# A two-layer transformer block: attention in equal chunks of 512 columns, and a mixture of experts that computes only the chosen token-expert pairs

## The chip, the cores and the metric

One core of one Trainium2 chip runs the whole program in one launch. The metric is the device time of one execution in microseconds (us), the median over several runs. Shapes: 8 batches of 512 tokens with 128 features, 16 heads of 8 features, 8 experts with 512 hidden units, two experts for each token.

## The reference, cut to what matters

```python
q, k1, k2, v = (split_heads(x @ W.T) for W in (Wq, Wk1, Wk2, Wv))
a = softmax(causal(q k1^T * SCALE)) - sigmoid(lam)[h] * softmax(causal(q k2^T * SCALE))
a = a / maximum(sum(abs(a), -1), 1e-6)
x = layernorm(x + merge_heads(a @ v) @ Wo.T)

xn = layernorm(x) * gamma + beta
w, idx = top_k(softmax(xn @ router_w.T / 1.5), 2)
wdense = sum(one_hot(idx, 8) * w[..., None], -2)
h = silu(einsum('btd,edf->betf', xn, W1))
y = einsum('betf,efd->betd', h, W2)
x = layernorm(x + einsum('bte,betd->btd', wdense, y) + x)
```

The reference computes all 8 experts for every token and weighs six of them with zero.

## The kernel before, in words

**One static order for each engine.** The kernel is written by hand, one instruction stream for each engine, with semaphores between them. `run` calls `body(b, stages)` for b from -1 to 9. In a body, every engine walks through 64 slots (`for slot in range(UNITS)`), and does in each slot what a lag of its own assigns to it. An engine executes in order, so a wait in one slot holds back all that stands behind it on that engine.

**Attention.** A unit is one head and one tile of 128 queries; its score strip is 128 to 512 columns wide (causal), so 16 heads x 4 tiles = 64 units a batch, one in each slot. PE writes the two score strips into PSUM (`scores`, two units deep; L853, and the causal mask by L855), DVE takes each strip's negated maximum (`neg_max`, L723), ACT takes the exponential with its row sum (L491), and POOL makes the difference of the two softmaxes in place: a scaling (L441) and then a subtraction (L445), for each unit. `inv_l2` (DVE L714) and `lam_l1` (POOL L437) are made once for four units. PE transposes the difference (L883), ACT copies it out of PSUM (`diffT`, L499), PE multiplies with the values (L872). DVE sums absolute values (`abs_sum`, L734, two units in one instruction), and every four units makes `guard` (L623) and its reciprocal (L740). Scores are stored as three bfloat16 parts: SP writes `parts` to DRAM (L390) and reads them back as `stack` (L398), nine transfers for each of four groups of heads, for the batch that follows.

**The rest of the layer in side slots.** `SIDE` gives slots to tasks. "prep" tasks are for batch b+1 (transpose of x, projections L773, values), "post" tasks for batch b-1: division, output projection, two norms, transposed `xnT`, router logits, 16 small routing steps on DVE (`route`), and then the experts: for each of 8 experts 4 `hidden` tasks (PE L803, one 128x512 product; ACT tanh L537; DVE `hT` L686) and 4 `expert` tasks (PE L809, 4 accumulating products of 128x128; DVE adds the gated result into `acc`, L698). An fp32 product is two PE instructions. Tasks of slots above 63 run as "late" in the body after. The weights of all experts lie in SBUF (4 MB, loaded once at L384). PSUM banks `side0` and `side1` alternate between the side tasks; in the last bodies, the four score banks join them.

**SP** issues all transfers, in this order in a body: x for the next batch, x for the residual, `parts`, `stack`, and the output. `stack` of group g waits until the scores of that group in the running batch are done.

Of the kernel before, what the change touches and what calls it, by code (L numbers as in the profile page):

```python
# [29 lines left out]
FP32, BF16 = mybir.dt.float32, mybir.dt.bfloat16  # L30
ALU, ACT, AX = mybir.AluOpType, mybir.ActivationFunctionType, mybir.AxisListType

B, T, D = 8, 512, 128
# [4 lines left out]
NF = F // P  # L38
UNITS = NH * NT
QUAD = 4  # L40
QUADS = UNITS // QUAD
NG = NH // QUAD
TILE_ORDER = (1, 0, 2, 3)
# [8 lines left out]
LAG_DIFF = QUAD + LAG_EXP  # L52
LAG_TRANS = LAG_DIFF + 2
LAG_COPY = LAG_TRANS + 1
LAG_ABS = LAG_DIFF + 2
LAG_DEN = LAG_ABS + 2
LAG_PV = LAG_COPY + QUAD
LAG_SIDE = 1

SIDE = {}
POST_SLOTS = {"spread": 8, "den_T": 9, "divide": 11, "out_proj": 13, "norm1": 15, "norm2": 18,
              "xn_T": 19, "logits": 21, "router_exp": 22}
FIRST_EXPERT_SLOT = 20
EXPERT_TASKS = (1, 2, 1, 1, 1, 1, 1, 1, 0, 1, 1, 1, 1, 1, 1, 1)
PREP_SLOTS = (24, 29, 36, 42, 43)


def tile_of(q):  # L70

    return TILE_ORDER[q % NT]


def _place():

    def put(slot, *task):
        SIDE.setdefault(slot, []).append(task)

    for name, slot in POST_SLOTS.items():  # L80
        put(slot, "post", name)
    tasks = []
    for e in range(E + 1):
        for n in range(NF):
            if e < E:
                tasks.append(("post", "hidden", e, n))
            if e:
                tasks.append(("post", "expert", e - 1, n))
    slot = FIRST_EXPERT_SLOT
    while tasks:  # L90
        for _ in range(min(EXPERT_TASKS[slot % len(EXPERT_TASKS)], len(tasks))):
            put(slot, *tasks.pop(0))
        slot += 1
    put(slot + 1, "post", "norm3")
    put(slot + 3, "post", "finish")
# [4 lines left out]
_place()  # L100
ROUTE_STEPS, ROUTE_PLACES = 16, 4
# [3 lines left out]
PSUM_TASKS = ("den_T", "out_proj", "xn_T", "logits", "hidden", "expert", "x_T", "proj", "values")  # L105

STORED = (0, 1, 2, 0, 1)
# [7 lines left out]
class Signal:  # L115


    def __init__(self, sem, per_batch, step=1):
        self.sem, self.per, self.step = sem, per_batch, step

    def after(self, batch, n):

        value = (batch * self.per + n) * self.step + CREDIT
        return max(value, 1) if isinstance(value, int) else value


def build(nc, x, wqT, wk1T, wk2T, wvT, woT, lam, gamma, beta, rwT, w1, w2, out):
    ctx = ExitStack()  # L130
    with ctx:
# [8 lines left out]
        def signal(name, per_batch, step=1):  # L140
            signals.append(Signal(ctx.enter_context(nc.semaphore(name)), per_batch, step))
            return signals[-1]

# [14 lines left out]
        w1_sb = sb("w1_sb", [P, E, F])  # L158
        w2_sb = sb("w2_sb", [P, E, NF, D])

# [8 lines left out]
        scratch = nc.dram_tensor("parts_dram", [3, NH, len(STORED), HD, T], BF16).ap()  # L169
        stack = sb("stack", [STACK, 3, NH, T], BF16)  # L170


        neg_max = sb("neg_max", [P, 2, QUAD, 2])
        sums = sb("sums", [P, 4, 2, QUAD])
        inv_l2 = sb("inv_l2", [P, 2, QUAD])
        lam_l1 = sb("lam_l1", [P, 2, QUAD])
        exps = sb("exps", [P, 2, 2, QUAD, T])
        diff = exps[:, :, 1, :, :]
        diffT = sb("diffT", [P, 2, QUAD, T])
        abs_sum = sb("abs_sum", [P, 2, QUAD])  # L180
        guard = sb("guard", [P, QUAD])
        inv_den = sb("inv_den", [P, NT, NH])
        inv_wide = sb("inv_wide", [P, NT, NH, HD])
# [5 lines left out]
        r1 = sb("r1", [P, NT, D])  # L189
        x1 = sb("x1", [P, NT, D])  # L190
# [14 lines left out]
        gates = sb("gates", [P, NT, E])  # L205
        tanh_sb = sb("tanh_sb", [P, 2, T])
        hT = sb("hT", [P, 2, NF, T])
        x1_twice = sb("x1_twice", [P, NT, D])
# [10 lines left out]
        CONSTS = 9 + E  # L219
        weights_in = ctx.enter_context(nc.semaphore("weights_in"))  # L220
        experts_in = ctx.enter_context(nc.semaphore("experts_in"))
# [16 lines left out]

        score_done = signal("score_done", 2 * UNITS)
        max_done = signal("max_done", 2 * UNITS)  # L240
        exp_done = signal("exp_done", 2 * UNITS)
        inv_l2_done = signal("inv_l2_done", QUADS)
        lam_l1_done = signal("lam_l1_done", QUADS)
        scaled_done = signal("scaled_done", UNITS)
        diff_done = signal("diff_done", UNITS)
        abs_done = signal("abs_done", 2 * QUADS)
        trans_done = signal("trans_done", UNITS)
        diffT_copied = signal("diffT_copied", UNITS)
        pv_done = signal("pv_done", QUADS)
        den_done = signal("den_done", 2 * QUADS)  # L250

        res_loaded = signal("res_loaded", 1, 16)
        post_psum = signal("post_psum", 4)
        expert_psum = signal("expert_psum", E * (NF + NT))
# [17 lines left out]
        tanh_done = signal("tanh_done", E * NF)  # L272
        hidden_done = signal("hidden_done", E * NF)
        expert_done = signal("expert_done", E * NT)
# [4 lines left out]
        def reader(task):  # L279
# [5 lines left out]
                "hidden": (hidden_done, NF * task[2] + task[3] + 1) if name == "hidden" else None,  # L285
# [28 lines left out]
        def psum_of(task):  # L314

            if task[1] in ("hidden", "expert"):
                return expert_psum
# [593 lines left out]
```

## Time and profile before

| what | us |
|---|---|
| median of 3 runs | 1229.79 (1222.33 to 1231.21) |
| the profiled execution, its device time | 1223.18 |
| its span in the trace | 1221.3 |
| PE, DVE, ACT, POOL busy | 1103.2, 1044.4, 915.2, 834.0 |

The span is what the hardware profiler saw from first to last instruction; 1.9 us of the execution lie around it. Instructions that wait on a semaphore, and those that issue a transfer, are not counted as busy.

### The profile page before, as it was taken

To read this page: it belongs to the slowest core of one execution; us is meant where nothing else is said; L and a number is where in the kernel's file an instruction comes from. 1 tells how busy PE (TensorE), PEld (TensorE's weight loads), DVE (VectorE), ACT (ScalarE), POOL (GpSimd) and SP (SyncE) were. 2 spreads that over 40 slices of the span, in tenths; PEclk is the share of its full clock that TensorE was granted. 3 is DMA by queue.
4 is the path that set the end of the run, shared out by engine and by line. 5 is a ranking of instruction groups with operands and counts; after the bars stand their busy time and mean duration, and the time that the engine had idled before them with its cause. 6 is when DMAs were issued, how large, how long until landed. Compare 5 with 4: busy or idle time off the path is not lost.

```text
span 1221.3 us, 29361 instructions
## 1 busy us (share of the span) xinstructions
PE 1103.2 (90%) x8786; PEld 725.7 (59%) x8786; DVE 1044.4 (86%) x2722; ACT 915.2 (75%) x2882; POOL 834.0 (68%) x1245
## 2 busy tenths in 40 slices
PE   3788869999899989999899997999899998999897
PEld 1355536666556655666556665666556665566565
DVE  1688788988999899999999899999999999898664
ACT  1688868888688877888688876888678886787232
POOL 2599976776768757877667776777677777677100
PEclk8577779999999999999999999999999999999899
DMA  7503400232005200142003300052002410000000
GB/s 213 126 14 80 99 1 3 62 82 48 1 14 118 70 2 2 36 110 57 1 14 86 89 15 1 21 125 57 1 2 57 89 48 1 19 1 2 1 10 9
DMA packets 62142, 54.66 MB, mean 45 GB/s; under 512 B 6050, under 2 KB 59938, under 8 KB 61986
## 3 DMA queue, kind: packets, MB, share of 16 engines
q1 hardware_dynamic: 61986, 52.78, 17.8%
q8 instruction: 73, 1.20, 0.4%
q14 instruction: 83, 0.68, 0.2%
HBM read 37.03 MB, written 15.73 MB: 43 GB/s over the span
## 4 chain that ended last, share of the span: by engine, by line
PE 66%; DVE 18%; issue 7%; POOL 4%; ACT 2%; SPq 1%; DMA 1%; DVEq 0%; POOLq 0%; ACTq 0%
PE side L809 14%; PE side L803 13%; PE trans L883 12%; PE scores L853 8%; PE heads L872 7%; DVE neg_max L723 6%; PE scores L855 4%; DVE abs_sum L734 3%; PE scores L803 2%; PE scores L809 2%; POOL exps L445 2%; PE side L773 2%; DVE hT L686 1%; DVE xh L566 1%; POOL exps L441 1%
## 5 line engine op out<-in xcount | busy, mean ns | idle before, releaser
L491 ACT ACTIVATE exps<-scores,neg_max 128x256 f32<-128x256 f32 (+3 forms) x1024 | 537.9, 529 | 97.5 <-DVE neg_max L723 80.8
L723 DVE TENSOR_REDUCE neg_max<-scores 128x1 f32<-128x256 f32 (+3 forms) x1024 | 448.7, 479 | 72.8 <-PE scores L855 69.3
L445 POOL TENSOR_TENSOR exps<-exps 128x384 f32<-128x384 f32 (+3 forms) x512 | 444.7, 868 | 42.7
L441 POOL TENSOR_SCALAR exps<-exps,inv_l,lam_l 128x384 f32<-128x384 f32 (+3 forms) x512 | 313.6, 613 | 141.2 <-DVE inv_l L714 138.4
L853 PE MATMUL scores<-stack 72*128 72x256 bf16 (+3 forms) x1024 | 274.1, 314 | 17.5 <-DMA stack<-parts_dram 13.5
L809 PE MATMUL side<-w_sb,hT 128*128 128x128 f32 x1816 | 253.6, 283 | 29.5 <-DVE acc L698 18.1
L883 PE MATMUL trans<-ident,exps 128*128 128x128 f32 x1280 | 254.9, 300 | 22.8 <-ACT diffT L499 19.4
L499 ACT ACTIVATE diffT<-trans 128x384 f32<-128x384 f32 (+3 forms) x512 | 223.4, 436 | 52.9 <-PE trans L883 52.1
L809 PEld LDWEIGHTS side<-w_sb,hT 128*128 128x128 f32 x1816 | 222.6, 192 | 63.7 <-DVE acc L698 29.9
L803 PE MATMUL side<-xnT,w_sb 128*128 128x512 f32 x458 | 247.2, 621 | 1.8 <-ACT xnT L526 1.0
L883 PEld LDWEIGHTS trans<-ident,exps 128*128 128x128 f32 x1280 | 150.4, 147 | 134.7 <-issue 102.5
L855 PE MATMUL scores<-causal_bf,ident_bf 128*128 128x128 bf16 x1024 | 216.5, 228 | 0.0
L491 ACT ACTIVATION_READ_ACCUMULATOR exps<-scores,neg_max 128x1 f32 x1024 | 210.7, 206 | 0.0
L734 DVE TENSOR_REDUCE abs_sum<-exps 128x2 f32<-128x512 f32 (+3 forms) x256 | 206.9, 808 | 1.7 <-POOL exps L445 1.7
L686 DVE SCALAR_TENSOR_TENSOR hT<-tanh_sb,side 128x512 f32<-128x512 f32 x229 | 155.8, 680 | 36.3 <-ACT tanh_sb L537 34.5
L537 ACT ACTIVATE tanh_sb<-side 128x512 f32<-128x512 f32 x229 | 136.1, 594 | 48.0 <-PE side L803 44.8
L853 PEld LDWEIGHTS scores<-stack 72*128 72x128 bf16 x1024 | 108.2, 106 | 64.1 <-ACT exps L491 22.8
L872 PE MATMUL heads<-diffT,v_sb 128*32 128x128 f32 x2560 | 139.2, 291 | 0.0
L872 PEld LDWEIGHTS heads<-diffT,v_sb 128*32 128x32 f32 x2560 | 51.0, 109 | 122.2 <-ACT diffT L499 61.4
L855 PEld LDWEIGHTS scores<-causal_bf,ident_bf 128*128 128x128 bf16 x1024 | 105.4, 103 | 7.7
L437 POOL TENSOR_TENSOR lam_l<-sums,lam_all 128x4 f32<-128x4 f32 x128 | 25.9, 203 | 91.1 <-ACT exps L491 90.7
L803 PEld LDWEIGHTS side<-xnT,w_sb 128*128 128x128 f32 x458 | 69.3, 191 | 15.0 <-DVE hT L686 2.7
(94 smaller groups left out, 685.2 us busy)
## 6 DMA issues: line engine op xcount, KB each, us to landing
stack<-parts_dram SPq DMA_DIRECT2D x288, 96.0 KB
parts_dram<-parts SPq DMA_DIRECT2D x104, 128.0 KB, 2.4
x_in<-x_dram SPq DMA_DIRECT2D x8, 256.0 KB, 4.5
w_sb<-w_dram SPq DMA_DIRECT2D x1, 2048.0 KB, 9.1
x_res<-x_dram SPq DMA_DIRECT2D x8, 256.0 KB, 4.5
o_dram<-y_out SPq DMA_DIRECT2D x8, 256.0 KB, 3.4
wq_sb<-wqT_dram SPq DMA_DIRECT2D x1, 64.0 KB
wq_sb<-wk1T_dram SPq DMA_DIRECT2D x1, 64.0 KB
```

The source lines that it names most:

```text
L441: nc.gpsimd.tensor_scalar(diff[:, q % 2, j, 0:w], exps[:, q % 2, 1, j, 0:w], inv_l2[:, q % 2, j:j + 1], lam_l1[:, q % 2, j:j + 1], ALU.mul ...
L445: nc.gpsimd.tensor_tensor(diff[:, q % 2, j, 0:w], diff[:, q % 2, j, 0:w], exps[:, q % 2, 0, j, 0:w], ALU.subtract).then_inc(diff_done.sem, 1)
L491: nc.scalar.activation(exps[:, q % 2, k, j, 0:w], scores[:, u % 2, k, 0:w], ACT.Exp, bias=neg_max[:, q % 2, j, k:k + 1], accum_out=sums[:, ...
L499: nc.scalar.activation(diffT[:, q % 2, j, 0:w], trans[:, 0:w], ACT.Copy)\
L723: nc.vector.tensor_reduce(neg_max[:, q % 2, j, k:k + 1], scores[:, u % 2, k, 0:w], AX.X, ALU.max, negate=True).then_inc(max_done.sem, 1)
L734: nc.vector.tensor_reduce(abs_sum[:, q % 2, j - 1:j + 1], diff[:, q % 2, j - 1:j + 1, 0:w], AX.X, ALU.add, apply_absolute_value=True).then ...
L803: last = nc.tensor.matmul(bank[:, :], w1_sb[:, e, f * P:(f + 1) * P], xnT[:, :], start=True, stop=True)
L809: last = nc.tensor.matmul(bank[:, 0:D], hT[:, e % 2, f, t * P:(t + 1) * P], w2_sb[:, e, f, :], start=(f == 0), stop=(f == NF - 1))
L853: nc.tensor.matmul(scores[:, u % 2, k, 0:w], stack[:, 0, QUAD * g + j, t * P:(t + 1) * P], stack[:, 1 + k, QUAD * g + j, 0:w], start=True, ...
L855: nc.tensor.matmul(scores[:, u % 2, k, w - P:w], ident_bf[:, :], causal_bf[:, :], start=False, stop=True).then_inc(score_done.sem, 1)
L872: last = nc.tensor.matmul(heads[k * STRIP:(k + 1) * STRIP, t * P:(t + 1) * P], v_sb[:, i, NG * k + g, :], diffT[:, q % 2, k, i * P:(i + 1) ...
L883: last = nc.tensor.transpose(trans[:, i * P:(i + 1) * P], diff[:, q % 2, j, i * P:(i + 1) * P], ident[:, :])
```

## The change

**Chunks.** A batch has 40 slots in place of 64. A slot holds a chunk of exactly 512 score columns: for each pair of heads five chunks, of widths 512; 384+128; 256+256; 512; 384+128. Exponentials, scalings and products stay one for each unit; the subtraction (POOL), the copy to `diffT` (ACT) and four transposes (PE) are now one set for each chunk. Rings are longer (`exps` 7 chunks, `diffT` 12).

**Experts.** Routing finds the two experts of each token. A token-expert pair gets a row in a buffer sorted by expert, in which each expert is padded to tiles of 128 rows: at most (1024 + 8 x 127) / 128 = 15 tiles, and always 15 are computed. POOL scatters the rows of `xh` to DRAM with 8 indirect transfers of 128 rows of 512 bytes, SP reads the sorted rows back, PE transposes them, each tile goes through one expert whose weights (512 KB) SP loads for that tile from DRAM (the expert's number is read from SBUF into a register), the result goes to DRAM, and POOL gathers it with 8 indirect transfers; DVE combines it with the gates. These stages have slots of their own up to slot 98, so that they run over three bodies: routing and scatter in the body after the batch's attention, tiles in the next, gather and end in the third.

```diff
+TOP = 2
+TILES = (TOP * T + E * (P - 1)) // P
+CHUNKS = [range(c, min(c + NT, TILES)) for c in range(0, TILES, NT)]
-LAG_DIFF = QUAD + LAG_EXP
-LAG_TRANS = LAG_DIFF + 2
+LAG_DIFF = 4
+LAG_TRANS = 4
-LAG_PV = LAG_COPY + QUAD
+LAG_PV = LAG_COPY + 1
+EXP_RING, DIFF_RING = 7, 12
+PAIR_CHUNKS = (((3, 0, 0),), ((2, 0, 0), (0, 0, 384)), ((1, 0, 0), (1, 1, 256)), ((3, 1, 0),), ((2, 1, 0), (0, 1, 384)))
+SUM_SETS = {1: (0, 3, 1), 2: (3, 8, 4), 4: (4, 7, 1)}
+POST_SLOTS = {"spread": 8, "den_T": 10, "divide": 10, "out_proj": 12, "norm1": 16, "norm2": 18, "xn_T": 21, "logits": 22, "router_exp": 24, "count": 30, "place": 31, "sorted": 44, "norm3": 95, "finish": 98}
+HIDDEN_SLOTS = (45, 47, 49, 51, 53, 55, 59, 61, 65, 67, 69, 71, 73, 75, 77)
+EXPERT_SLOTS = (48, 50, 52, 54, 56, 58, 62, 64, 68, 70, 72, 74, 76, 77, 79)
+WEIGHT_SLOTS = (41, 43, 45, 47, 49, 51, 55, 57, 61, 63, 65, 67, 69, 70, 70)
+TURN_SLOTS = (44, 52, 58, 68)
+Y_OUT_SLOTS = (57, 65, 72, 82)
+SCATTER_SLOTS = (31, 32, 33, 34, 35, 36, 37, 38)
+GATHER_SLOTS = (82, 83, 85, 85, 86, 88, 89, 90)
+COMBINE_SLOTS = (86, 87, 88, 89, 90, 91, 92, 93)
+STACK_SLOT = 33
 @block.sync
+                if name == "sorted":
+                    sp.wait_ge(scattered.sem, scattered.after(n, TOP * NT))
+                    for c in CHUNKS:
+                        sp.dma_start(xg[:, c[0]:c[-1] + 1, :], ...).then_inc(sorted_in.sem, 16)
+                if name == "weights":
+                    sp.wait_ge(expert_psum.sem, expert_psum.after(m, psum_count[("post", "expert", used)]))
+                    which = sp.value_load(owner_int[0:1, n % 2, j:j + 1], min_val=0, max_val=E - 1)
+                    sp.dma_start(w12_sb[:, i % WEIGHTS_AHEAD, :], w12[bass.ds(which, 1), :, :]...)
-                    if isinstance(b, int) and b == -1:
-                        for dst, src in ((w1_sb[:, :, :], w1.rearrange("e d f -> d e f")), ...
-                            sp.dma_start(dst, src).then_inc(experts_in, 16)
+            sp.wait_ge(consts_made, CONSTS)
+            for i in range(2):
+                sp.dma_start(pools(x_sorted[i]), xg[:, :, :]).then_inc(sorted_cleared, 16)
 @block.gpsimd
-                        nc.gpsimd.tensor_tensor(diff[:, q % 2, j, 0:w], diff[:, q % 2, j, 0:w],
-                                                exps[:, q % 2, 0, j, 0:w], ALU.subtract).then_inc(diff_done.sem, 1)
+                        nc.gpsimd.tensor_tensor(diff[:, ring, :], diff[:, ring, :], exps[:, ring, 0, :], ALU.subtract)\
+                            .then_inc(diff_done.sem, 1)
+                        if name == "scatter":
+                            nc.gpsimd.indirect_dma_start(
+                                x_sorted[n % 2][:, :], bass.IndirectOffsetOnAxis(ap=place_int[:, n % 2, i:i + 1], axis=0),
+                                xh[:, i % NT, :], None).then_inc(scattered.sem, 16)
+                        if name == "gather":
+                            if i == 0:
+                                for s in range(2):
+                                    pool.wait_ge(y_sorted_out[s].sem, y_sorted_out[s].after(n, len(CHUNKS) // 2))
+                            nc.gpsimd.indirect_dma_start(y_back[:, i, :], None, y_dram[n % 2][:, :], ...)
 @block.vector
+                        if name == "combine":
+                            nc.vector.scalar_tensor_tensor(
+                                out=acc[:, t, :], in0=y_back[:, i, :], scalar=gates[:, n % 2, i // NT, t:t + 1],
+                                in1=acc[:, t, :] if i >= NT else x1_twice[:, n % 2, t, :], ...)
+                        for i, many, w, place, step in reductions(c):
+                            nc.vector.tensor_reduce(abs_sum[...], diff[:, ring_e(n, c), col:col + many * w]..., AX.X, ALU.add, ...)
 @block.tensor
+                if name == "turn":
+                    pe.wait_ge(sorted_in.sem, sorted_in.after(n, len(CHUNKS)))
+                    for i, j in enumerate(c):
+                        last = nc.tensor.transpose(bank[:, i * P:(i + 1) * P], xg[:, j, :], ident[:, :])
-                    last = nc.tensor.matmul(bank[:, :], w1_sb[:, e, f * P:(f + 1) * P], xnT[:, :], start=True, stop=True)
+                    for f in range(NF):
+                        last = nc.tensor.matmul(bank[:, f * P:(f + 1) * P], w12_sb[:, w, f * P:(f + 1) * P],
+                                                xgT[:, j // NT % 2, j % NT, :], start=True, stop=True)
```

A `hidden` task is now one whole tile (4 products of 128x128, tanh and `hT` of 128x512), an `expert` task one tile (4 products, and a 128x128 copy on ACT to `y_sorted`). ACT also copies each group of up to four transposed tiles (`turn`). New on DVE and PE are the tasks `count` and `place` (a few small products and seven small DVE instructions) that turn the routing into row numbers. `guard` and its reciprocal are now made twice a batch, for 32 units. DVE slots have a lag of 1 behind the table, POOL slots a lag of 2.

## Rows read from the trace of the kernel before

**Rows 1.** The page: busy time of each engine, and the shares of the chain

```profile
PE 1103.2 (90%) x8786; PEld 725.7 (59%) x8786; DVE 1044.4 (86%) x2722; ACT 915.2 (75%) x2882; POOL 834.0 (68%) x1245
...
PE 66%; DVE 18%; issue 7%; POOL 4%; ACT 2%; SPq 1%; DMA 1%; DVEq 0%; POOLq 0%; ACTq 0%
```

**Rows 2.** Windows: length, PE, PEld, DVE, ACT, POOL busy, clock, DMA share, GB/s

```profile
90.00:120.00 30.00, 26.29 (x202) 15.53 (x201) 25.68 (x58) 25.35 (x86) 27.25 (x40) 0.78 0.27 70
...
252.00:256.00 4.00, 4.00 (x39) 3.13 (x38) 3.76 (x11) 3.69 (x13) 3.83 (x5) 1.00 0.86 179
...
417.00:557.30 140.30, 132.22 (x1098) 88.09 (x1098) 129.72 (x342) 114.11 (x362) 103.97 (x154) 1.00 0.18 44
```

**Rows 3.** Instructions on `stack`: count, ns min/median/max, first and last start

```profile
L853 PE MATMUL scores<-stack x1024: 219/326/634, 37.9 to 1116.5; 72*128 72x256 bf16 x43, 72*128 72x384 bf16 x43, 72*128 72x512 bf16 x43, 72*128 72x128 bf16 x42
L398 SPq DMA_DIRECT2D stack<-parts_dram x288: 290/375/1662, 30.9 to 981.6; - x144
```

**Rows 4.** Timeline of POOL and SP: `v_sb` cleared, x issued as a batch's scores end

```profile
1.46 1.79 POOL L419 MEMSET v_sb<- 128x2048 f32 x1
...
7.88 0.40 SPq L375 DMA_DIRECT2D x_in<-x_dram  x1
...
143.85 0.40 SPq L375 DMA_DIRECT2D x_in<-x_dram  x1
...
278.22 0.39 SPq L375 DMA_DIRECT2D x_in<-x_dram  x1
```

**Rows 5.** Groups by shape, 417 to 557.3 us: count | busy us, mean ns | idle

```profile
L809 PE MATMUL side<-w_sb,hT 128*128 128x128 f32 x256 | 35.7, 282 | 3.9 <-DVE acc L698 3.0 <-issue 0.8
L803 PE MATMUL side<-xnT,w_sb 128*128 128x512 f32 x64 | 34.5, 621 | 0.0
...
L686 DVE SCALAR_TENSOR_TENSOR hT<-tanh_sb,side 128x512 f32<-128x512 f32 x33 | 22.4, 679 | 3.1 <-ACT tanh_sb L537 2.9
...
L723 DVE TENSOR_REDUCE neg_max<-scores 128x1 f32<-128x512 f32 x32 | 20.4, 678 | 0.2 <-PE scores L855 0.2
L445 POOL TENSOR_TENSOR exps<-exps 128x512 f32<-128x512 f32 x16 | 20.4, 1272 | 1.3
...
L698 DVE SCALAR_TENSOR_TENSOR acc<-side,gates,acc 128x128 f32<-128x128 f32 x28 | 9.5, 339 | 0.7 <-PE side L809 0.6
...
L723 DVE TENSOR_REDUCE neg_max<-scores 128x1 f32<-128x128 f32 x32 | 7.6, 279 | 2.3 <-PE scores L855 2.1
...
L623 DVE SCALAR_TENSOR_TENSOR guard<-sums,abs_sum 128x4 f32<-128x4 f32 x17 | 7.2, 425 | 0.0
...
L445 POOL TENSOR_TENSOR exps<-exps 128x128 f32<-128x128 f32 x16 | 7.3, 455 | 1.3
...
L464 POOL TENSOR_TENSOR rstd<-var_eps,minus_half 128x4 f32<-128x4 f32 x3 | 3.1, 1018 | 0.2
```

**Rows 6.** Timeline, 415.9 to 417.2 us: DVE's `guard` beside POOL's subtraction

```profile
416.05 1.00 POOL L445 TENSOR_TENSOR exps<-exps 128x384 f32<-128x384 f32 x1
...
416.34 0.73 DVE L623 SCALAR_TENSOR_TENSOR guard<-sums,abs_sum 128x4 f32<-128x4 f32 x1
```

**Rows 7.** The chain that ended last, in the tail: start, us, what

```profile
1152.40 1.50 PE side L796 x8
...
1175.65 0.89 PE scores L809 x8
1176.54 0.86 PE scores L803 x2
...
1218.07 0.51 DVE y_out L566 x2
```

**Rows 8.** The page: transfers, KB each, us from issue to landing

```profile
stack<-parts_dram SPq DMA_DIRECT2D x288, 96.0 KB
...
x_in<-x_dram SPq DMA_DIRECT2D x8, 256.0 KB, 4.5
w_sb<-w_dram SPq DMA_DIRECT2D x1, 2048.0 KB, 9.1
...
o_dram<-y_out SPq DMA_DIRECT2D x8, 256.0 KB, 3.4
```

More of the change, by code:

```diff
@@ L81, in _place @@
         put(slot, "post", name)
[L82 to L95, printed above, removed]
+    for name, slots in (("weights", WEIGHT_SLOTS), ("turn", TURN_SLOTS), ("hidden", HIDDEN_SLOTS),
+                        ("expert", EXPERT_SLOTS), ("y_out", Y_OUT_SLOTS), ("scatter", SCATTER_SLOTS),
+                        ("gather", GATHER_SLOTS), ("combine", COMBINE_SLOTS)):
+        for i, slot in enumerate(slots):
+            put(slot, "post", name, i)
     for n, slot in enumerate(PREP_SLOTS):
@@ L104 @@
 PREP_TASKS = [t for s in sorted(SIDE) for t in SIDE[s] if t[0] == "prep"]
-PSUM_TASKS = ("den_T", "out_proj", "xn_T", "logits", "hidden", "expert", "x_T", "proj", "values")
+PSUM_TASKS = ("den_T", "out_proj", "xn_T", "logits", "count", "place", "turn", "hidden", "expert",
+              "x_T", "proj", "values")
+EXPERT_PSUM = ("turn", "hidden", "expert")
 STORED = (0, 1, 2, 0, 1)
@@ L287, in reader @@
+                "expert": (y_copied, task[2] + 1) if name == "expert" else None,
             }[name]
[L290 to L297 removed]
@@ L309, in build @@
             for experts in (False, True):
-                chosen = [t for t in tasks if t[1] in PSUM_TASKS and (t[1] in ("hidden", "expert")) == experts]
+                chosen = [t for t in tasks if t[1] in PSUM_TASKS and (t[1] in EXPERT_PSUM) == experts]
                 for n, t in enumerate(chosen):
@@ L475, in body @@
             def body(b, stages):
-                for slot in range(UNITS):
+                for slot in range(SLOTS):
                     for k in range(2):
-                        for n, u in units(b, stages, slot, LAG_EXP):
-                            q, j = divmod(u, QUAD)
-                            w = (tile_of(q) + 1) * P
+                        for n, c in chunks(b, stages, slot, LAG_EXP):
+                            ring = ring_e(n, c)
+                            m, used = earlier(n, c, EXP_RING)
@@ new lines, in body @@
+                                act.wait_ge(abs_done.sem, abs_done.after(m, REDUCTIONS[used + 1]))
+                            act.wait_ge(max_done.sem, max_done.after(n, maxima_done(c, k)))
+                            for i, (t, _, _, col, place) in enumerate(units_of(c)):
+                                w = (t + 1) * P
+                                nc.scalar.activation(exps[:, ring, k, col:col + w], scores[:, c % 2, k, col:col + w],
+                                                     ACT.Exp, bias=neg_max[:, c % 2, k, i:i + 1],
+                                                     accum_out=sums[:, k, place:place + 1]).then_inc(exp_done.sem, 1)
@@ L500, in body @@
+                        for n, c in chunks(b, stages, slot, LAG_COPY) if k == 0 else ():
+                            m, used = earlier(n, c, DIFF_RING)
+                            act.wait_ge(trans_done.sem, trans_done.after(n, c + 1))
+                            act.wait_ge(pv_done.sem, pv_done.after(m, pv_done_for(used)))
+                            nc.scalar.activation(diffT[:, ring_d(n, c), :], trans[:, :], ACT.Copy)\
                                 .then_inc(diffT_copied.sem, 1)
-                    for task, n, bank in side_tasks(b, stages, slot):
+                    for task, n, bank in side_tasks(b, slot):
@@ new lines, in body @@
+                    for n, c in chunks(b, stages, slot, LAG_DEN):
+                        if (c + 1) % (SLOTS // 2) == 0:
+                            i = (c + 1) // (SLOTS // 2)
+                            half = slice((i - 1) * UNITS // 2, i * UNITS // 2)
+                            dve.wait_ge(den_done.sem, den_done.after(n, 2 * i - 1))
+                            nc.vector.reciprocal(inv_den[:, half], guard[:, half]).then_inc(den_done.sem, 1)
+                    if slot == V_SLOT and "attention" in stages:
```

762 lines of the change are left out of this document (467 added, 295 removed).

## The prediction, written before the result was known

> **What bounds the kernel now.** I read the page first. PE is busy for 90% of the span and DVE for 86%, and the chain that ended last lies for 66% on PE and 18% on DVE [rows 1]. Then the window of one batch in the steady part: of 140.3 us PE is busy 132.2, DVE 129.7, ACT 114.1, POOL 104.0, at full clock, with the transfers at 18% [rows 2]. So PE and DVE share the bound. Each is used at 92 to 94%, about what in-order engines that wait for each other reach here. A batch ends when its last scores are made: scores start at 37.9 us and the last are at 1116.5 [rows 3]. SP issues x for the next batch after nine `stack` transfers that wait for those scores (9 x 0.375 = 3.4 us). From its issues at 143.85 and 278.22 [rows 4], batch 0 took 102 us, batch 1 134 us, and batches 2 to 7 (1116.5 - 274.8) / 6 = 140.3 us each. The rest is 37.9 us of start and 104.8 us of tail. I cost the change in these four pieces.
>
> **PE.** `hidden` and `expert` are busy 34.5 + 35.7 = 70.2 us a batch [rows 5]. A 128x512 product pair takes 0.86 us and eight 128x128 instructions 0.89 us back to back [rows 7]. A new tile needs 8 + 8 instructions, 1.78 us; 15 tiles take 26.7 us. The routing pads to 15 tiles whatever the data, so this saving is sure. Turning 15 tiles and the small products of `count` and `place` add some 6 us, and full-width transposes neither save nor add 3. PE falls from 132 to about 132 - 70 + 27 + 6 = 95 us, with room for interrupted pipelining up to 100.
>
> **DVE.** Removed: 17 of 32 `hT` at 0.68 (11.6 us), 32 `acc` at 0.34 (10.9), 14 of 16 `guard` (7.2 - 0.9 = 6.3), and as many short reciprocals (2). `guard` is a small operation that takes 0.43 us on average [rows 5], and the timeline says why: it began at 416.34 and ended at 417.07, with POOL's subtraction, which ran from 416.05 to 417.05 [rows 6]. An operation of DVE with two SBUF inputs waits until POOL's instruction ends. Added: 8 `combine` of 128x128 with two SBUF inputs, 0.34 each and a wait of about 0.4 (up to 1.27, POOL's longest, in the bound): 6 us. A reduction has a fixed part: 279 ns for 128 columns and 678 for 512 [rows 5] leave 0.15 us. `abs_sum` goes from 32 to 56 instructions (+3.5), `neg_max` from 128 to 112 (-2.3). More `inv_l2`, `place` and `spread`: +4. Sum: 129.7 - 30.8 + 11.2 = 110 us. At the share of before (0.925) DVE alone would allow 119 us a batch.
>
> The Trainium skill (SBUF — State Buffer, "SBUF: two separate sides") calls the port pair of DVE and GpSimd an exclusive lock, held for the whole instruction; the trace's 0.73 us agree. It adds that an indirect transfer issued on GpSimd cannot write its descriptors while DVE holds the pair. No row here shows that; it would add to the price of an issue, and by it the slower rival below gains.
>
> **ACT.** 17 tanh and 24 smaller copies of `diffT` fewer, 15 short copies and 4 of `turn` more. Even its 114 us of before [rows 2] would bind nowhere below.
>
> **POOL.** Busy 104.0 us, and between scaling and subtraction it waits for itself, 0.08 us (idle before L445 1.3 us for 16) [rows 5]: occupied 109. The subtractions keep their columns and lose 24 fixed parts. 455 ns for 128 columns and 1272 for 512 give 0.18 us fixed: -4.4 us, and 24 self-waits -1.9. `lam_l1` 8 times more: +2. That is 104.5 us. Then come 16 indirect transfers. No row shows one. From below, an issue on SP takes 0.29 us at the least and 0.40 for x; from above, the longest issue of SP is 1.66 [rows 3, 4]. POOL's own small instruction of some work (`rstd`) takes 1.02 us [rows 5]. Since POOL has to read 128 indices and write 128 descriptors for each, I take 1.2 us, nearer to the last two: 19 us. So POOL needs 104.5 + 19 = 123.7 us, more than any other engine. In batch 0, which has hardly any side work, POOL was busy 27.25 of 30 us [rows 2]. With its self-waits (12 pairs, 1 us) that is a share of 0.95. **POOL becomes the bound, and the period 123.7 / 0.95 = 130 us.** It cannot be hidden: `turn`, `diffT`, `abs_sum` and the exponentials' ring all wait on POOL's differences within a few slots. Ends: 0.40 gives 111 / 0.95 = 117, so DVE's 119; 1.66 gives 131 / 0.95 = 138.
>
> The Trainium skill (DMA: Bandwidth & Descriptors, "Latency and other measured facts") gives about 1 us to first byte for a transfer issued on GpSimd, against 0.6 on SP. As an estimate from that page, an issue of 1.0 us makes the sum 126.6 us instead of 130.
>
> **SP and the transfers.** SP's new work is 15 weight loads, 4 sorted loads and 4 stores of results. 2048 KB of weights landed after 9.1 us [rows 8], so 512 KB need some 2 to 4 us, and 15 of them 35 us of a period whose transfers now take 18%. Loads go four tiles ahead; I cost them at nothing in the steady part. One place is tight. The sorted load (983 KB; small-row traffic runs at 179 GB/s [rows 2], 5.5 us) stands on SP behind the stack of group 3 (9 x 96 KB [rows 8], 4.8 us), x twice (3 us) and two weight loads (4 us), all issued after the batch's last scores. It lands about 19 us after them, and PE's first `turn` stands in slot 4, which with 3.2 us a slot comes at 13 us. PE then holds scores back for about 6 us; PE has 30 us of room, DVE and ACT have a slot of work, so 3 us stay, and while POOL is the bound they are inside its slack. I put 0 in the forecast and 7 in a rival.
>
> **The start.** The 4 MB of expert weights are no longer loaded, but x was ahead of them (issued at 7.88 us [rows 4]), and the parts went out at SP's own pace. New ahead of x: SP waits for POOL's constants (13 more, one nearly the size of the 1.79 us for `v_sb` [rows 4]: 1 us past the 7.88) and clears two buffers, 2 MB through the same queue, 8 us at 250 GB/s and 11 at the 179 of the small rows. First scores move from 37.9 to 47 us (42 to 52).
>
> **The batches.** Batch 0 has POOL's saving of 4.3 us: 98 us. Batch 1 has no experts yet, only the scatter: (104.5 + 9.6) / 0.95 = 120. Batch 2 has experts and scatter, no gather: 121. Batches 3 to 7: 5 x 130 = 650. Sum 989, against 1078.6.
>
> **The tail.** Before, it had one batch's experts on PE at 1.75 us a step and ended with y at 1218 [rows 7]. New, three stages run one behind the other. From the last scores to the end of the last batch's routing: logits came at 1152.4, so 36 us, and routing 8 more; `count` and `place` 3: 47 us (the 15 tiles of the batch before fit beside it, 15 x 2.2). Eight scatters 9.6, landing 2.5, sorted load 7: 66. Fifteen tiles with their loads at 2.2 to 2.4 us: 35, +3 for `turn`: 104. Store 3.4, eight gathers 9.6, landing 2.5: 119. Combine, norm, store [rows 8]: 8. So 127 us, 22 more than before.
>
> Sum: 47 + 989 + 127 = 1163 us of span, against 1221.3; with 1.9 us around it 1165, against 1223.2. The median of the runs lies 6.6 us above the profiled execution, so I predict **1168 us** for the median: -5%.
>
> **The rivals.**
> - *Cheap issues.* At 0.4 us, POOL needs 111 us and DVE binds with 119: batches 3 to 7 lose 55 us, batches 1 and 2 14, the tail 13: 1086. For it: SP's rows. Against: POOL makes them itself. 22%.
> - *PE's `turn` stalls everything* on the late sorted load: 7 us a batch in six batches, 1210. For it: the order on SP above. Against: PE's room. 13%.
> - *PE loses its clock.* In batch 0 the granted clock was 0.78 although PE was busy 26.3 of 30 us [rows 2], and with 95 us of work it idles more than before. At 0.78, 95 us take 122, and at a share of 0.92 the period is 133, with the norm chains slower: 1190. 10%.
> - *Slower: the issue of an indirect transfer on POOL.* Each 1 us on it costs 16 / 0.95 = 17 us in five batches, 8 / 0.95 in two, 16 in the tail: 117 us. The change loses everything at 1.2 + 62 / 117 = 1.73 us an issue. At 2.2 us the time is 1285. For it: the trace has nothing like it, and locks from DVE add. Against: no issue in the trace exceeds 1.66. 17%.
> - *It doesn't do what it says*: only if the sorted path waited so long that each batch ran alone; the slots are a whole body apart. Under 1%.
>
> **How the numbers follow.** The forecast keeps 37%, over issues of 0.9 to 1.6 us: 1133 to 1215 as its own range. To hold 8 in 10 the range takes in most of the cheap case and the slower one's first third: 1085 to 1248. A measurement of this kernel tells about 1% from no change, 1217 to 1242. Faster by over 1%: 37 + 22 + 13 + 10, less 6 for their upper ends, is 76%; same 7%; slower 17%.
>
> **What would show it.** In the profile after, the steady period by the distance of x's issues: 130 us. POOL's idle between instructions shrinks except where it issues transfers, and its gaps at the gathers and scatters give the price: 1.2 us. PE busy near 95 to 100 of 130, DVE near 110. First scores at 47, 127 us after the last. I am wrong if DVE is above 95% and POOL waits (cheap issues), if PE waits on `xg` for several us each batch, if the clock in the steady part is below 0.9, or if POOL's gap for one issue is 1.7 us or more.

## The result, and the profile after

The changed kernel takes 1194.16 us, the median of 4 runs (1191.83 to 1201.04), against 1230.5 for the kernel before (4 runs): a ratio of 0.972, 95% interval 0.968 to 0.976. So it is 2.8% faster where 5% were forecast; 1194 lies in the likeliest case's own range (1133 to 1215). The profiled execution has a span of 1199.3 us.

The page of the changed kernel: busy time of each engine, clock, chain, the two groups of indirect transfers, and three kinds of transfers.

```profile
PE 927.8 (77%) x8522; PEld 738.7 (62%) x8522; DVE 924.3 (77%) x2393; ACT 851.7 (71%) x2706; POOL 948.1 (79%) x1257
...
PEclk9577788669998898989898898979998788978797
...
POOL 34%; DVE 22%; PE 19%; issue 12%; ACT 6%; DMA 5%; SPq 2%; DVEq 0%; POOLq 0%; ACTq 0%
...
L639 POOL DMA_INDIRECT y_back<-y_sorted_dram,place_int x64 | 64.7, 1011 | 43.2 <-issue 41.7
L630 POOL DMA_INDIRECT x_sorted_dram<-xh,place_int x64 | 68.7, 1074 | 37.5 <-DVE owner_int L915 27.6
...
w_sb<-w_dram SPq DMA_DIRECT2D x120, 512.0 KB, 3.7
...
x_sorted_dram<-xg SPq DMA_DIRECT2D x2, 960.0 KB, 5.5
...
y_back<-y_sorted_dram,place_int POOLq DMA_INDIRECT x64, 2.7
```

PE and DVE led before [rows 1]; now POOL is first in busy time and in the chain, and nobody is over 80%.

The four pieces, from the first and last scores and from SP's issues of x, as for before [rows 3, 4]:

```profile
L1090 PE MATMUL scores<-stack x1024: 219/326/634, 41.7 to 1061.8; 72*128 72x384 bf16 x85, 72*128 72x512 bf16 x43, 72*128 72x256 bf16 x43
```

SP's issues of x, from its timeline (start, us, queue, line):

```profile
10.14 3.41 SPq L532 DMA_DIRECT2D x_in<-x_dram  x1
...
143.44 0.39 SPq L532 DMA_DIRECT2D x_in<-x_dram  x1
...
261.48 0.39 SPq L532 DMA_DIRECT2D x_in<-x_dram  x1
...
387.23 0.41 SPq L532 DMA_DIRECT2D x_in<-x_dram  x1
...
796.13 0.41 SPq L532 DMA_DIRECT2D x_in<-x_dram  x1
```

| piece, us | before | forecast | measured |
|---|---|---|---|
| until the first scores | 37.9 | 47 | 41.7 |
| batch 0 | 102.5 | 98 | 98.3 |
| batch 1 | 134.4 | 120 | 118.0 |
| batch 2 | 140.3 | 121 | 125.8 |
| batches 3 to 7, each | 140.3 | 130 | 135.6 |
| last scores to the end | 104.8 | 127 | 137.5 |
| span | 1221.3 | 1163 | 1199.3 |

(For example, batch 1 is 261.48 - 143.44; batches 3 to 7 are (1061.8 + 3.4 - 387.23) / 5. The 140.3 of before is the mean of batches 2 to 7.) From the third batch on, each is 5 us longer than forecast; that and the tail are the whole difference, less 5 us at the start.

Windows of the changed kernel: one steady batch as a whole. The columns are those of [rows 2].

```profile
520.40:657.00 136.60, 111.76 (x1065) 90.61 (x1065) 115.78 (x298) 105.80 (x338) 117.95 (x153) 0.90 0.41 121
```

The same batch in tenths:

```profile
520.40:534.00 13.60, 8.09 (x48) 5.72 (x52) 7.45 (x18) 8.98 (x31) 12.61 (x16) 0.62 0.78 224
534.00:547.70 13.70, 10.93 (x150) 8.46 (x143) 12.16 (x30) 11.24 (x38) 12.53 (x17) 1.00 0.44 143
...
561.40:575.00 13.60, 12.12 (x136) 10.30 (x140) 12.05 (x31) 9.87 (x33) 12.59 (x17) 1.00 0.28 80
...
602.30:616.00 13.70, 13.47 (x156) 9.89 (x154) 12.97 (x34) 11.41 (x36) 10.56 (x15) 1.00 0.57 171
616.00:629.60 13.60, 10.91 (x91) 8.96 (x90) 13.16 (x33) 11.21 (x40) 10.63 (x15) 0.87 0.20 62
629.60:643.20 13.60, 13.60 (x108) 12.04 (x108) 9.58 (x28) 9.20 (x31) 11.08 (x13) 0.75 0.28 89
```

Up to 588 us POOL is busy 12.5 of 13.6 us, as a bound would be. From there to 643 us it is down to 10.4 to 11.1; first DVE is busy for 13 of 13.7 us (12.97, 13.16), with PE above it in one of these slices (13.47), and then PE is busy without a gap, at a clock of 0.75, while DVE falls to 9.58. So the leader changes inside a batch. Whether a leader's load also sets the time is for the experiments.

### The profile page after: what moved, and what is told of

Its sections match the earlier page's. It is cut to its first block, busy times and chain, and to the rows that moved or that the text cites. A ratio compares the mean times of both kernels' runs of the same rounds, so it can differ in the third digit from the quotient of the medians.

```text
span 1199.3 us, 27952 instructions
## 1 busy us (share of the span) xinstructions
PE 927.8 (77%) x8522; PEld 738.7 (62%) x8522; DVE 924.3 (77%) x2393; ACT 851.7 (71%) x2706; POOL 948.1 (79%) x1257
## 4 chain that ended last, share of the span: by engine, by line
POOL 34%; DVE 22%; PE 19%; issue 12%; ACT 6%; DMA 5%; SPq 2%; DVEq 0%; POOLq 0%; ACTq 0%
POOL exps L614 13%; POOL exps L610 11%; DVE neg_max L962 7%; POOL x_sorted_dram L630 4%; PE trans L1124 4%; ACT exps L680 4%; POOL y_back L639 3%; DVE abs_sum L972 3%; PE scores L1090 3%; PE side L1067 3%; PE side L1073 3%; POOL lam_l L604 1%; DVE stats L760 1%; DMA xg<-x_sorted_dram 1%; DVE hT L924 1%
## 5 line engine op out<-in xcount | busy, mean ns | idle before, releaser
L680 ACT ACTIVATE exps<-scores,neg_max 128x512 f32<-128x512 f32 (+3 forms) x1024 | 539.2, 541 | 74.8 <-DVE neg_max L962 72.7
L962 DVE TENSOR_REDUCE neg_max<-scores 128x1 f32<-128x512 f32 (+3 forms) x896 | 424.6, 526 | 79.4 <-PE scores L1092 75.1
L614 POOL TENSOR_TENSOR exps<-exps 128x512 f32<-128x512 f32 x320 | 406.5, 1270 | 26.7
L610 POOL TENSOR_SCALAR exps<-exps,inv_l,lam_l 128x512 f32<-128x512 f32 (+3 forms) x512 | 312.4, 616 | 59.1 <-DVE inv_l L953 42.1
L1090 PE MATMUL scores<-stack 72*128 72x512 bf16 (+3 forms) x1024 | 279.9, 343 | 15.5 <-DMA stack<-parts_dram 14.9
L972 DVE TENSOR_REDUCE abs_sum<-exps 128x1 f32<-128x512 f32 (+3 forms) x448 | 224.6, 525 | 67.6 <-POOL exps L614 67.2
L687 ACT ACTIVATE diffT<-trans 128x512 f32<-128x512 f32 x320 | 194.4, 608 | 95.2 <-PE trans L1124 93.8
L1073 PE MATMUL side<-w_sb,hT 128*128 128x128 f32 x824 | 120.0, 291 | 21.5 <-DVE hT L924 21.5
L1067 PE MATMUL side<-xgT,w_sb 128*128 128x128 f32 x784 | 122.4, 305 | 1.2 <-DMA w_sb<-w_dram 1.1
L1073 PEld LDWEIGHTS side<-w_sb,hT 128*128 128x128 f32 x824 | 105.0, 200 | 28.4 <-DVE hT L924 24.0
L639 POOL DMA_INDIRECT y_back<-y_sorted_dram,place_int x64 | 64.7, 1011 | 43.2 <-issue 41.7
```

The source lines that it names most:

```text
L610: nc.gpsimd.tensor_scalar(diff[:, ring, col:col + w], exps[:, ring, 1, col:col + w], inv_l2[:, i:i + 1], lam_l1[:, i:i + 1], ALU.mult, ALU ...
L614: nc.gpsimd.tensor_tensor(diff[:, ring, :], diff[:, ring, :], exps[:, ring, 0, :], ALU.subtract)\
L680: nc.scalar.activation(exps[:, ring, k, col:col + w], scores[:, c % 2, k, col:col + w], ACT.Exp, bias=neg_max[:, c % 2, k, i:i + 1], accum ...
L687: nc.scalar.activation(diffT[:, ring_d(n, c), :], trans[:, :], ACT.Copy)\
L962: nc.vector.tensor_reduce(neg_max[:, c % 2, k, i:i + many], scores[:, c % 2, k, col:col + many * w].rearrange("p (i w) -> p i w", w=w), AX ...
L972: nc.vector.tensor_reduce(abs_sum[:, place:place + (many - 1) * step + 1:step], diff[:, ring_e(n, c), col:col + many * w].rearrange("p (i ...
```

## The experiments

All are changes of the changed kernel, except e8. "Ratio" is to the kernel before, which ran beside each; where they are compared with the changed kernel, its 1194 are from a run of their own.

**e1: POOL's 16 issues on SP.**

```diff
-  nc.gpsimd.indirect_dma_start(x_sorted[n % 2][:, :], IndirectOffsetOnAxis(place_int...), xh[:, i % NT, :], None)
+  sp.dma_start(x_sorted[n % 2][i * P:(i + 1) * P, :], xh[:, i % NT, :])      # gathers likewise
```

> The changed kernel, with its 16 indirect transfers a batch replaced by plain transfers of the same bytes, issued by SP, to and from fixed rows (the placing of rows by expert is left out; all other work stays). Theory A, POOL's issues are on the path in the whole steady part: they take 16 x 1.29 us a batch in the trace of the changed kernel (from the end of one POOL operation to the start of the next); without them POOL needs 104 of 136 us, DVE binds with 116 busy, the period falls from 136.4 to about 125, and with 12 us off the tail the time falls from 1194 to 1115 (1100 to 1135). Theory B, the 9% of the period in which POOL is idle come from engines waiting for each other and not from POOL's load: the period falls by 3 us at most, the time is 1165 to 1180.

Measured: 1165.46 us, ratio 0.949 (0.942 to 0.956). SP's issues of x (517.12, 646.60) give a period of 129.5 there. The time is at the lower edge of theory B, the period lies between the two. One load was late: PE waited for the sorted rows at a `turn`, 16.6 us in two waits within 200 us (waits of e1, 500 to 700 us: in total, times, longest).

```profile
PE side L1057 <- DMA xg<-x_sorted_dram: 16.6, 2, 8.4
```

**e5: the same, with that late load moved earlier.**

```diff
-"sorted": 44,   SCATTER_SLOTS = (31, 32, 33, 34, 35, 36, 37, 38)
+"sorted": 38,   SCATTER_SLOTS = (31, 31, 31, 31, 31, 31, 31, 31)
```

> As e1 (the 16 transfers issued by SP, to and from fixed rows; the placing by expert is left out), but all eight stores of rows stand on SP ahead of the stack of the next batch, and the load of the sorted rows ahead of the stack's last group. In e1 the period was 130.5 us, PE waited up to 8.4 us a batch for these rows at the first turn, and in the 13 us at the start of a batch PE and DVE were nearly idle. Theory A (POOL's issues cost a batch some 14 us, and e1 hid half of that behind a late load): the period falls to 121 to 124, the time to 1165 - 6 x 7.5 = 1120 (1105 to 1135). Theory B (the issues cost no more than e1 showed, DVE binds at 130): 1155 to 1165.

Measured: 1156.99 us, ratio 0.938 (0.933 to 0.943). That is in the range of theory B, though its reason, DVE as the bound, is not shown by it (DVE is busy 88% of the second batch). Windows of e5, two batches:

```profile
387.36:522.00 134.64, 112.71 (x1065) 91.06 (x1065) 114.68 (x296) 105.18 (x338) 99.90 (x137) 0.89 0.45 127
522.00:651.40 129.40, 106.72 (x1065) 86.30 (x1065) 113.74 (x299) 105.14 (x338) 100.57 (x138) 0.93 0.47 132
```

POOL lost 17.4 us of busy time (117.95 to 100.57), is busy 78% of a batch and cannot be the bound; the period went down by 7 us only (135.6 to 128.8, from the third batch to the last scores). So of each microsecond that POOL's issues take, at least 0.4 reach the period. It is "at least", because e5 is not clean either: PE waits for the rows no longer than in the changed kernel, but now for a load of weights, in every batch (waits of e5, 500 to 640 us).

```profile
PE side L1065 <- DMA w_sb<-w_dram: 5.4, 1, 5.4
```

From the third batch on these waits sum to 21 us, 4.2 a batch; the changed kernel, e1 and e7 below have none. One stall was traded for another of half the size. SP, which works in order, has 16 more issues among its loads here; that these delay the weights is argued, not shown. If all 4.2 us came back, the period would be 124.6 and the time about 1136 (an estimate), at the edge of theory A. So e5 puts the price of POOL's issues between 7 and 11 us of the period, and does not decide how A would fare without any late load.

**e7: less work for DVE.** One maximum serves both exponentials; the second is left out. The softmax is mathematically the same with any shift, as long as the second strip's scores neither exceed the first strip's maximum by so much that the exponential overflows, nor lie so far below it that all of a row's exponentials vanish.

```diff
-                        for k in range(2):
+                        for k in range(1):
...
-                                                     ACT.Exp, bias=neg_max[:, c % 2, k, i:i + 1],
+                                                     ACT.Exp, bias=neg_max[:, c % 2, 0, i:i + 1],
```

> The changed kernel, in which DVE takes only the maximum of the first score strip, and ACT shifts both exponentials by it (the second maximum is left out; 25 us less for DVE a batch, nothing less for POOL). Theory A (POOL's issues alone set the period of 136.4): 1194 within 6 us. Theory C (POOL and DVE each bind part of a batch, and each hides most of what is taken from the other): POOL alone remains, its 125 us at 0.97 are a period of 129, the time is 1194 - 7 x 7 = 1145 (1135 to 1160).

Measured: 1157.35 us, ratio 0.942 (0.938 to 0.947). POOL keeps all its work and the time falls all the same, so "POOL alone" is out; the time lies in the range of theory C. It is 3% below the changed kernel, and the fastest version that keeps the whole layer, at the price of the narrower range of scores. With its own waits and the gaps of its issues (6.4 us a batch, worked out below), POOL is occupied 0.96 to 0.97 of the period here (the window of e7 below), against 0.91 in the changed kernel: once DVE has room, POOL does come close to a bound.

**e10: e5 and e7 together.**

> e5 and e7 together: POOL without its 16 issues (fixed rows, the placing left out) and DVE without the second maximum. e5 alone took 37 us off. Theory C: the two together take off far more than the sum of each alone, since nothing is left that binds at 129; the next bound is ACT's 106 us or PE's work at its low clock, 112 busy: period 115 to 120, time 1050 to 1090. Theory D (the period of 129 in e5, 129.5 in the kernel before without experts, is the latency of a loop over the engines and no engine's load): e10 stays within 15 us of the better of e5 and e7, 1125 to 1150.

Measured: 1114.89 us, ratio 0.909 (0.905 to 0.913). Windows of e7:

```profile
390.00:520.00 130.00, 110.86 (x1073) 89.45 (x1070) 90.36 (x242) 105.55 (x339) 119.23 (x154) 0.91 0.46 129
```

And of e10:

```profile
380.00:504.00 124.00, 106.01 (x1046) 85.98 (x1042) 92.41 (x239) 101.42 (x328) 98.27 (x134) 0.93 0.48 137
```

e5 takes 37 us off 1194, e7 37, both 79. They add, to within the scatter of the runs. A bound of one engine would make the second relief worth nothing or everything, and neither happened: with 17 us less on POOL and 22 less on DVE the distance of x's issues is 125, with PE, the busiest, at 86% of it. Both C and D miss. PE's waits for weights are in e10 too (20 us from the third batch on, 4 a batch), so what is next after POOL and DVE cannot be read from it.

**e2 and e3: other places for the issues.**

```diff
+SCATTER_SLOTS = (31, 31, 32, 32, 33, 33, 34, 34)          # e2
+GATHER_SLOTS = (82, 82, 83, 83, 84, 84, 85, 85)
+SCATTER_SLOTS = (31, 32, 33, 35, 36, 38, 39, 41)          # e3, expert tables + 2
+GATHER_SLOTS = (83, 85, 86, 88, 89, 91, 92, 94)
```

> The changed kernel, with the eight scatters and the eight gathers each in four neighbouring slots, two in a slot. Theory A1, POOL is behind all through a batch, so the place of its issues doesn't matter: 1194 within 6 us. Theory A2, POOL falls behind only in the slots with issues and the other engines are then starved, while elsewhere POOL waits for them: two bursts of 10.3 us in four slots outrun the one slot of slack (3.4 us), about 5 us more for each burst than now, and the time rises by 8 x 6 to 1220 to 1245.

> The changed kernel, with the scatters over 11 slots in place of 8 and the gathers over 12 in place of 9, and the tables of the expert stages shifted by two slots to make room. Theory A1 (place of issues is without effect): 1194 within 6 us. Theory A2 (uneven load): each batch saves 2 to 5 us, 1194 - 8 x 3.5 = 1166 (1155 to 1180). If the shift costs more than the spreading gives, 1194 to 1205.

Measured: e2 1212.95 us, ratio 0.985 (0.979 to 0.991); e3 1219.78 us, ratio 0.990 (0.985 to 0.995). e2's last scores come at 1079.9 (the changed kernel: 1061.8), its tail is 6 us shorter. Bursts cost 18 us in the steady part, less than A2 wanted. e3's last scores are at 1062.5: spreading gives nothing in the steady part. What e3 loses lies behind them, where 151 us pass in place of 137.5. A2 is wrong for e3, and A1 for e2; neither time lies in a range that was given for it.

**e6: gathers in the second half of a batch**, where POOL has time.

```diff
+GATHER_SLOTS = (83, 86, 89, 92, 95, 98, 101, 104)
+COMBINE_SLOTS = (87, 90, 93, 96, 99, 102, 105, 108)      # norm3 and finish 15 slots later
```

> The changed kernel with its gathers three slots apart from slot 83 to 104 in place of nine neighbouring slots, and the combining behind them; x1_twice and the gates three deep for it. In the changed kernel POOL is busy 92% in the first half of a batch and waits for DVE in the second, where the norms and the routing stand. Theory A2 (each half has its own bound): gathers in the second half use POOL's idle time there, the period falls from 136.4 to 131 (128 to 133) and the time from 1194 to 1165, if DVE's combining doesn't undo it. Theory A1 (the place of the issues is without effect, as e3 had it in the steady part): 1194 within 8 us.

Measured: 1209.21 us, ratio 0.981 (0.977 to 0.985). That is 15 us above 1194, outside both ranges. The profiled execution has its first and last scores at 43.2 and 1061.9: nothing gained. It is the fastest of the six (1199.59), so it doesn't show where the rest went. Reading the tenths above as two halves with a bound each, to be filled up, was not borne out.

**e4: more work for PE**, two of four transposes made twice.

```diff
-                        for i in range(NT):
+                        for i in [0, 1, 0, 1, 2, 3]:
```

> The changed kernel, in which PE makes two of the four transposes of each chunk twice (the same values again), 14 us more work a batch for PE, nothing more for the others. If PE is off the path, as the forecast had it: 1194 within 8 us, with the clock in the steady part above 0.90. If PE's latency is part of the loop (PE waits for POOL at the transposes, then DVE waits for the scores behind them): half of it appears, 1194 + 8 x 7 = 1250 or more. If the low clock had cost time and the added work raises it to 1.0: 1194 or below, down to 1180.

Measured: 1203.02 us, ratio 0.977 (0.971 to 0.983): 9 us more. The added work is less than the 14 us a batch of the expectation: at full clock, six transposes back to back take 0.87 us where four take 0.65 (timelines, from 602 us), so 40 sets add 9 us a batch, some 70 us in all. PE's busy time rose by only 24 us (927.8 to 952.1): the mean clock is 0.905 against 0.86, and PE's other work took less time (the first products of a tile 294 ns each in place of 306). So much of the addition came back with the higher clock, and what was left costs 9 us. That is no proof that PE's load is free.

**e11: some of DVE's work on ACT.**

```diff
+                            if c % KINDS == 3:
+                                nc.scalar.activation(abs_out[:, :], diff[:, ring_e(n, c), :], ACT.Abs,
+                                                     accum_out=abs_sum[:, place:place + 1])
...
+                                nc.scalar.activation(y_out[:, t, :], acc[:, t, :], ACT.Identity,
+                                                     bias=shift[:, t:t + 1], scale=rstd[:, 2, t:t + 1])
```

> The changed kernel, complete, with some of DVE's work on ACT, which is busy 78%: the absolute sum of every fifth chunk, and the last normalisation (7.5 us less for DVE a batch, 7 us more for ACT). Theory C: DVE binds for about 55 of 136 us, so 2 to 4 us a batch are won and the time is 1165 to 1180. If POOL alone binds: 1194 within 6. If ACT's added work sits in the loop between scores and differences: above 1200.

Measured: 1203.56 us, ratio 0.980 (0.977 to 0.983). DVE's busy time fell by 4.5 us a batch, ACT's rose by 6.6, and the steady period fell by 1.4 us (three distances of x's issues: 134.9 in place of 136.3) to 2.0 (to the last scores at 1055.6). That is at the lower end of what theory C wanted, but the start is 2 us longer, the tail 3.5 us, and the median 9 us above 1194. The work is exchanged, not removed, and nothing of the gain is left in the whole.

**e8 and e9: both kernels without their experts.** e8 is the kernel before without the `hidden` and `expert` tasks and the load of their weights; e9 is the changed kernel without everything from `count` to `combine`. The last norm reads twice x1 in both.

```diff
-                tasks.append(("post", "hidden", e, n))          # e8, and "expert"
-"count": 30, "place": 31, "sorted": 44,                        # e9, and the nine tables
```

> The kernel before without its expert products (hidden and expert tasks and the load of the weights left out; the last norm reads twice x1). POOL is occupied 109 us a batch and binds: period 113 to 116, time 965 to 1000. So the dense experts cost some 245 us in the kernel before.

> The changed kernel without its expert path (count, place, scatter, sorted load, turn, hidden, expert, result store, gather, combine and the two cleared buffers left out; the last norm reads twice x1). If chunks alone are what gained: POOL needs 104 us in place of 109, period 107 to 110, time 925 to 950, 35 to 45 us below the kernel before without its experts, and then the sorted path costs about 250 us, no less than the dense one. If the sorted path is what gained: the two kernels without experts lie within 15 us of each other.

Measured: e8 1076.18 us, ratio 0.869 (0.864 to 0.874); e9 942.88 us, ratio 0.763 (0.760 to 0.766). Windows of e8:

```profile
500.00:600.00 100.00, 77.15 (x587) 46.48 (x585) 81.45 (x222) 73.00 (x248) 78.81 (x117) 0.72 0.17 39
600.00:700.00 100.00, 78.72 (x624) 48.10 (x623) 78.99 (x205) 76.14 (x260) 85.48 (x124) 0.76 0.25 58
```

And of e9:

```profile
500.00:600.00 100.00, 76.93 (x722) 54.05 (x714) 91.93 (x239) 83.88 (x280) 92.28 (x125) 0.81 0.25 62
```

This is the largest surprise. Without experts the two differ by 133 us, with them by 36. e9 came as expected (period 109, POOL and DVE at 92%). e8 has a period of 129.5 (its x issues: 524.33, 653.30) and no engine over 86% in either window. So the dense experts, 70 us of PE a batch, cost the kernel before 1234 - 1076 = 158 us in all (1234.2 is its median beside e8), and the sorted path costs the changed one 1194 - 943 = 251.

**e12: is it the longer ring?**

```diff
-EXP_RING, DIFF_RING = 7, 12
+EXP_RING, DIFF_RING = 5, 12
```

> e9 (the changed kernel without its expert path, 943 us) with the ring of exponentials 5 chunks long in place of 7, so 2560 columns, as many as the eight units of the kernel before hold. The kernel before without its experts took 1076 us at a period of 129.5, with no engine busy over 85%. If the longer ring is what the chunks gain (theory R), the period rises from 109 to 120 or more and the time to 1025 or more. If it is the equal size and the smaller number of chunks, hand-overs between engines 40 times a batch in place of 64 (theory H), the time stays at 943 to 960.

Measured: 945.71 us, ratio 0.768 (0.764 to 0.773), 3 us over e9. Theory R falls. Equal chunks and fewer hand-overs remain, argued and not shown. Three other differences were not tried: the longer ring of `diffT` (12 chunks in place of 8 units), the sums for which POOL waits (four units at a time before, one or two chunks now), and the other slots of the norms and the routing.

## Why the prediction was right, and where it was off

**The price of an indirect transfer** was the unknown on which most hung; I took 1.2 us between 0.29 and 1.66. The timeline of POOL in the changed kernel:

```profile
520.46 1.26 POOL L614 TENSOR_TENSOR exps<-exps 128x512 f32<-128x512 f32 x1
521.88 1.08 POOL L630 DMA_INDIRECT x_sorted_dram<-xh,place_int  x1 [0.16 <-issue]
523.01 1.09 POOL L610 TENSOR_SCALAR exps<-exps,inv_l,lam_l 128x384 f32<-128x384 f32 x2
```

From the end of the subtraction (521.72) to the next start 1.29 us pass. The slower rival wanted 1.73 and is out, and the cheap rival (0.4) too. The Trainium skill (DMA: Bandwidth & Descriptors, "Latency and other measured facts") gives about 1 us to first byte for this path and puts it down to the emission of descriptors. The 1.01 and 1.07 us of the issues are of that size; no row here shows the first byte.

**The loads.** POOL needs 117.95 busy, 40 self-waits of 0.08 and 16 x 0.2 around the issues: 124.4 us (forecast 123.7). PE is busy 111.8 at a clock of 0.90, which I estimate as 101 us at full clock (95 to 100). DVE is at 115.8 (110): the `combine` were cheaper than put down (3.9 for 6), but `neg_max` rose by 1.7 instead of shrinking by 2.3, the cast of `parts` took 3.3 in place of 1.3, and a few small routing steps 1.7 more. Together that is 5.6 us. The norms are not among them (5.7 us, 5.9 before). Groups of the same batch:

```profile
L936 DVE SCALAR_TENSOR_TENSOR acc<-y_back,gates,acc 128x128 f32<-128x128 f32 x4 | 2.5, 624 | 0.0
...
L936 DVE SCALAR_TENSOR_TENSOR acc<-y_back,gates,x_twice 128x128 f32<-128x128 f32 x4 | 1.4, 362 | 0.0
```

Same shape, 624 or 362 ns on average. One routing step of 128x32 shows why: it began at 622.33, took 1.15 us where its like took 0.21 before, and ended at 623.48, with POOL's subtraction, which ran from 622.16 to 623.43. That agrees with the lock in the Trainium skill (SBUF — State Buffer, "SBUF: two separate sides"): the price is a matter of what runs on POOL at the moment.

**The step that failed** is "POOL becomes the bound, and the period 123.7 / 0.95 = 130 us". The load was right to 1 us (124.4 for 123.7); the share was 0.91 in place of 0.95. I took 0.95 from batch 0, in which POOL stood alone with hardly any side work. In the steady part DVE is at 116 of 136, PE at 112 and ACT at 106, each of them waits in order for the others, and POOL does not reach 0.95. e7 shows this directly: with 25 us off DVE and all of POOL's work kept, POOL reaches 0.96 and the period is 129.3, the forecast's 130. And e5, e7 and e10 show that POOL's load is not the only one that counts: 17 us off POOL give 7 us a batch (with PE's new waits for weights in it), 25 us off DVE give 6, and both give 14 to the last scores, or 11 by the distance of x's issues (5.0 and 5.5 for each alone by that measure). The step costs 5 to 6 us a batch, 31 us in all.

**The attribution was off as well.** I gave equal chunks 4.3 us a batch (POOL's fixed parts) and looked to PE's relief for the gain. By e8 and e9 the two kernels lie 133 us apart when there are no experts, and the sorted path costs 93 us more on the changed kernel (251) than the dense one does on the kernel before (158). Right for batch 0 (98.3 against 102.5), the 4.3 us is far too little once side work runs (e9's 109 against e8's 129.5). The forecast had it the other way: 8 x 4.3 = 34 us from the chunks and the rest of its 62 us from the experts. By this reckoning one term was much too small and the other had the wrong sign, and they offset each other: that the total came out 26 us from the forecast is in part luck. The reckoning has a gap, though: the chunks with dense experts were never run, so what the chunks are worth there, and what the sorted path is worth on top of them, is not shown, and the cause of the net gain of 36 us stays argued.

**The start**: x was issued at 10.14 us, and scores began at 41.7 in place of 47. The two cleared buffers (960 KB each) landed after 5.5 us; I had priced them at the rate of small rows, 179 GB/s, and from 10 to 16 us the transfers moved 348 (windows of 2 us).

**The tail** was 10 us longer than forecast. Its chain:

```profile
1122.57 0.48 PE scores L1067 x5
...
1124.31 0.30 issue
1124.61 0.95 POOL x_sorted_dram L630
...
1131.17 5.09 DMA xg<-x_sorted_dram
1136.39 1.09 PE scores L1059 x4
...
1157.78 4.66 DMA w_sb<-w_dram
...
1172.61 2.26 DMA y_sorted_dram<-y_sorted
1174.87 6.04 issue
1180.91 1.01 POOL y_back L639
...
1189.79 2.54 DMA y_back<-y_sorted_dram,place_int
```

First `turn` 74.6 us after the last scores (forecast 66): the routing shares PE and DVE with the tiles of the batch before and with their loads. The tiles take until about 1178, 42 us (38), and three loads of weights stand in the chain with 4.4 to 5.0 us each from issue to landing. PE itself idled for them only 4.3 us in five waits. In the steady part of the changed kernel it never waited for them, as forecast; in e5 and e10 it did. Scatter, gather, combine and end came as worked out.

**The other rivals.** PE waited for the sorted rows 2.3 us in the steady batch, not 7 (in e1, 8.4, where the rows leave by SP). The clock did fall, from 1.00 to 0.90 in the steady part, down to 0.75 in the stretch where PE was busy throughout; e4 shows that added work raised the clock again; what the low clock costs by itself was not measured.

What stays open: why the kernel before without experts stands at 129.5 us, and what the sorted path costs beyond POOL's issues and DVE's work. In 200 us of e8, PE's transposes waited 28.9 us for ACT's copies and DVE 28.0 us for scores, in e9 22.3 and 12.1 (waits, 500 to 700 us): engines that wait for each other, with no bound among them. Equal chunks with dense experts were not tried. The two prices (943 + 158 = 1101) may not simply be added there: full-width transposes save PE nothing, so PE would keep about the 132 us a batch of before [rows 2], and the period could hardly fall below that.

## What to carry to other kernels

When four engines are each busy 78 to 87% of a batch in one static order, no single load divided by a share gives the period. Removing a microsecond from DVE gave 0.25 us, and from POOL 0.4 or somewhat more. Moving work between engines gave at most 2 us a batch, moving it in time nothing, and neither made the whole faster. Take work away rather than shift it, and expect a quarter to a half of it. After each relief, look again for a wait that it has brought in, as the load of weights in e5. A change with two parts should be measured with each part alone: here the chunks were measured without experts (133 us) but not with the dense ones, and so their share in the 36 us is not known.

## What was not expected of the hardware

An indirect transfer of 128 rows of 512 bytes holds POOL for 1.29 us in a stream and for 1.26 when they stand back to back (0.96 + 0.30 in the tail), gather and scatter nearly alike (1.01 and 1.07), and a gather landed 2.7 us after its issue. Two clears of 960 KB, issued one behind the other, landed 5.5 us after their issue, with 348 GB/s while they ran, twice as fast as the small-row traffic before [rows 2]. And SP's own issue of x behind them took 3.41 us in place of 0.40.
